# Bias row sums: scaling on the scalar engine, summing by accumulating DMAs, one addition on the vector engine

## The chip, the cores and the metric

The kernel runs on one core of a Trainium2 chip. The metric is the device time of one execution in microseconds (us), the median over several runs. A profile of one further execution gives the start and duration of every instruction on the tensor engine (PE for its matmuls, PEld for its weight loads), the vector engine (DVE), the scalar engine (ACT), GpSimd (POOL) and the sync engine (SP, which here only issues DMAs), and of the DMA queues.

## What is computed

Two layers are applied to 4096 tokens of width 1024. In each, a first linear map (`cond`) feeds a second one (`ffn`) with low-rank experts, and the result is added to the input:

```python
x = x + _L0_ffn_ref(_L0_cond_ref(x, ...), ...)      # layer 0: weight rounded to a codebook, then W_base, b_base, experts
x = x + _L1_ffn_ref(_L1_cond_ref(x, ...), ...)      # layer 1: weight, bias, adapter per sequence, then base_W, experts

# inside _L0_ffn_ref
base = xf @ W_base.T + b_base
# inside _L1_cond_ref
base = jnp.einsum('bsi,oi->bso', x, weight) + bias
# inside _L1_ffn_ref
base = jnp.einsum('bsd,od->bso', x, base_W)
logits = jnp.einsum('bsd,ed->bse', x, router_W)
```

All linear maps between the two layers' non-linear parts are folded into products of weight matrices first, and the tokens are sent through the folded matrices. Folding also needs the two biases pushed through the matrices behind them: with M the 1024 x 1160 matrix `m1t` (base_W, the experts' A and the router of layer 1) and E the 1024 x 1288 matrix of the first folding stage, the kernel needs the row vector

`bias_sum = sum over r of bias1[r] * M[r, :] + sum over r of bias0[r] * E[r, :]`

with M's columns put at their places among E's. These are the "bias row sums".

## The kernel before, in words

Every float32 matrix product is done as three products of a high and a low part (`split_product`, L555 to L559); ACT makes a high part (`hi_of`), DVE the low part (`lo_of`). The order of the work on each engine is written out by hand, and semaphores tie the engines together. The stages, by the time at which they stand in the trace:

- 0 to 162 us: the product E, and beside it the rounding of layer 0's weight. E is stored chunk by chunk (128 rows) to `e_scratch` in device memory.
- 162 to 221 us, the C stage: for j = 0 to 7 and two halves h of 512 columns, a 1024-long product of a block of `wall` with `weff` (`c_product`) goes to one of 8 PSUM banks; ACT copies it out as `c0_hi` (the tile `c_hi` in the trace), DVE as `c0_lo` (`c_lo`). Blocks 13 to 16 of `wall` (needed by j = 4 to 7) are split by ACT and DVE behind j = 0, 1, 4 and 5 (`W_AFTER`, `w_split`: `w_hi`, `w_lo`).
- 221 to 239 us, the H stage: eight groups of matmuls, i = 0 to 7 (L725). Into groups 4 to 7 are put 22 small matmuls (eleven pairs) with a column of ones (`bias_sum`, L708) that sum `bacc` over its 128 partitions. Group 4 therefore waits for `bacc` to be finished, and it waits for `h_sum`, the first of DVE's additions `h_add` (L1672), as group i waits for the addition of group i - 4 for its PSUM bank.
- 239 to some 355 us, the G stage: further products of the folded matrices; the first reads `en_hi` and `en_lo`, made from `en_raw`, which SP loads from `e_scratch` when the bias sums are finished, since `en_raw` lies over the buffer `ea`.
- The rest: the tokens, in 16 tiles of 256.

The bias sums are made during the C stage. For each of 8 chunks k of 128 rows, POOL loads 128 rows of M into the one buffer `ma` and 128 rows of E into the one buffer `ea`. DVE multiplies each row with its bias (one number per partition) and adds it to `bacc`, [128 x 1288]: two instructions for `ma` (L1651 with 1024 columns, L1652 with 136), one for `ea` (L1656). POOL loads the next chunk when DVE has read the last one. On DVE the chunks stand behind j = 2 (one), 3 (two), 4 (one), 5 (two) and 6 (two). Behind them come the two `c_lo` of j = 7, then `b0t_lo` (the low part of another weight), then the `h_add`s.

Of the kernel before, what the change touches and what calls it, by code (L numbers as in the profile page):

```python
# [65 lines left out]
def build(nc, xq, wall, m1t, aallt, x0t, b0t, lb1, lorabt, loraa, wq, cbook, ids, packed, out,  # L66
          e_dram, p1_dram, b_dram, t_dram, p0_dram):
    with ExitStack() as ctx:
# [5 lines left out]
        def at(name, shape, dt, offset):  # L74
            return nc.alloc_sbuf_tensor_at(name, shape, dt, offset=offset)
# [53 lines left out]
        ea = at("ea", [P, NE], F32, r4 + 33280)  # L129
        ma = at("ma", [P, NM1], F32, r4 + 46880)  # L130
# [141 lines left out]
        ld_ma, ld_ea, ma_ok, mb_ok = sem("ld_ma"), sem("ld_ea"), sem("ma_ok"), sem("mb_ok")  # L272
# [13 lines left out]
        zero_ok, ids_ok = sem("zero_ok"), sem("ids_ok")  # L286
# [18 lines left out]
        fin_ok, fin_mm = sem("fin_ok"), sem("fin_mm")  # L305
# [23 lines left out]
        def _(sp):  # L329
# [55 lines left out]
            sp.wait_ge(mb_ok, KC)  # L385
# [105 lines left out]
        def _(pool):  # L491
# [12 lines left out]
            pool.dma_start(ma[:], m1t[0:P, :]).then_inc(ld_ma, 16)  # L504
# [4 lines left out]
            pool.dma_start(ea[:], e_dram[0:P, :]).then_inc(ld_ea, 16)  # L509
# [43 lines left out]
        def _(pe):  # L553
# [536 lines left out]
        def _(act):  # L1090
# [348 lines left out]
        def _(v):  # L1439
# [197 lines left out]
            nc.vector.memset(bacc[:], 0.0).then_inc(zero_ok, 1)  # L1637
# [6 lines left out]
            def bias(k):  # L1644
                v.wait_ge(ld_ma, 16 * k + 16)
                if k:
                    v.wait_ge(mb_ok, k)
                else:
                    v.wait_ge(zero_ok, 2)
                b = b1c[:, k:k + 1]  # L1650
# [3 lines left out]
                v.wait_ge(ld_ea, 16 * k + 16)  # L1654
                v.wait_ge(ma_ok, k + 1)
# [546 lines left out]
```

## Time and profile before

| | |
|---|---|
| median of 3 runs | 899.62 us (899.13 to 900.24) |
| the profiled execution, its own time | 899.72 us |
| its span from first to last instruction | 898.0 us |
| PE busy | 891.7 us (99%) |
| DVE busy | 673.5 us (75%) |
| ACT busy | 327.5 us (36%) |
| POOL busy | 149.1 us (17%) |
| TensorE clock granted | the highest digit in all 40 slices |

"Busy" is the share of the span in which an engine has an instruction under way. PE is busy nearly throughout, so an instruction on another engine matters where PE comes to wait for it. 1.7 us of the profiled execution lie outside its span.

### The profile page before, as it was taken

Reading aid. Unit: us, or ns where it says so; the run is one execution under the profiler, and the core shown is the slowest. Engines: PE = TensorE matmul, PEld = TensorE weight load, DVE = VectorE, ACT = ScalarE, POOL = GpSimd, SP = SyncE. Lnnn points to the kernel's source line nnn. Section 1 sums busy time; section 2 is a strip of 40 time slices with the busy share of each in tenths; the row PEclk is TensorE's granted clock in tenths of the full one; section 3 lists DMA queues with packets and bytes.
Section 4 is the critical chain, followed back from the end, with each engine's and each line's share of the span. In section 5 each row is a group of like instructions: output and inputs, shape, how many; then the busy total and the mean of one; then the engine's idle time right before and its main releaser. Section 6 shows DMA issues by size and latency. Waiting matters only on the chain.

```text
span 898.0 us, 13642 instructions
## 1 busy us (share of the span) xinstructions
PE 891.7 (99%) x4641; PEld 780.5 (87%) x4641; DVE 673.5 (75%) x1473; ACT 327.5 (36%) x546; POOL 149.1 (17%) x298
## 2 busy tenths in 40 slices
PE   8999999999999999999999999999999999999998
PEld 8999998888998888888888888888888888888887
DVE  7899899675687868888676776776776776767764
ACT  6578778411334424232322222222222222222220
POOL 0100010011002001414212312212302302302300
PEclk9999999999999999999999999999999999999999
DMA  9523330666412042575787887887887887886875
GB/s 361 194 89 109 121 127 24 215 228 201 143 51 93 2 141 83 190 278 186 233 288 244 300 298 245 293 299 247 295 284 260 299 293 246 302 292 242 304 271 207
DMA packets 61123, 192.52 MB, mean 214 GB/s; under 512 B 7777, under 2 KB 10874, under 8 KB 59134
## 3 DMA queue, kind: packets, MB, share of 16 engines
q1 hardware_dynamic: 50332, 160.04, 50.3%
q0 software_dynamic: 10432, 31.35, 11.6%
q8 instruction: 37, 0.61, 0.3%
q10 hardware_dynamic: 290, 0.26, 0.1%
q14 instruction: 32, 0.26, 0.1%
HBM read 159.39 MB, written 32.76 MB: 214 GB/s over the span
## 4 chain that ended last, share of the span: by engine, by line
PE 85%; DVE 6%; DMA 5%; ACT 2%; issue 1%; SPq 0%; DVEq 0%; ACTq 0%
PE bank L924 30%; PE bank L557 11%; PE bank L558 11%; PE bank L559 11%; PE bank L906 6%; PE bank L892 4%; DMA ea<-e_scratch 3%; PE bank L901 2%; PE bank L1017 2%; DVE bacc L1656 1%; DMA w_raw<-wall 1%; DVE rbuf L1611 1%; PE bank L725 1%; DMA m_raw<-m1t 1%; PE bank L835 1%
## 5 line engine op out<-in xcount | busy, mean ns | idle before, releaser
L924 PE MATMUL bank<-g_hi,xs 128*128 128x512 f32 x448 | 152.6, 398 | 0.0
L528 POOL DMA_DIRECT2D p1sel<-p_scratch x128 | 65.3, 510 | 340.2 <-issue 340.0
L924 PE MATMUL bank<-t_hi,xs 128*128 128x512 f32 x328 | 108.7, 392 | 0.0
L924 PEld LDWEIGHTS bank<-g_hi,xs 128*128 128x128 f32 x448 | 83.2, 188 | 15.6
L924 PE MATMUL bank<-g_lo,xs 128*128 128x512 f32 x224 | 88.3, 394 | 0.0
L1450 DVE TENSOR_TENSOR xs<-x_raw,xs 128x1024 fp32r<-128x1024 f32 x60 | 73.3, 1244 | 12.2 <-ACT xs L1093 11.9
L557 PE MATMUL bank<-gx,xs 128*128 128x304 f32 x256 | 78.5, 307 | 0.0
L559 PE MATMUL bank<-gx,xs 128*128 128x304 f32 x256 | 77.4, 302 | 0.0
L1093 ACT ACTIVATE xs<-x_raw 128x1024 fp32r<-128x1024 f32 x60 | 61.7, 1053 | 42.5 <-PE bank L924 41.8
L558 PE MATMUL bank<-gx,xs 128*128 128x304 f32 x256 | 77.2, 301 | 0.0
L924 PEld LDWEIGHTS bank<-t_hi,xs 128*128 128x128 f32 x328 | 61.6, 188 | 14.2 <-DMA t_lo<-t_scratch 0.5
L924 PE MATMUL bank<-t_lo,xs 128*128 128x512 f32 x164 | 64.0, 390 | 0.0
L1611 DVE SCALAR_TENSOR_TENSOR rbuf<-qbuf,thr,rbuf 128x1024 f32<-128x1024 f32 x48 | 59.5, 1281 | 5.0 <-ACT rbuf L1144 4.4
L557 PE MATMUL bank<-m_hi,w_hi 128*128 128x388 f32 (+1 forms) x184 | 63.0, 343 | 0.0
L558 PE MATMUL bank<-m_lo,w_hi 128*128 128x388 f32 (+1 forms) x184 | 62.3, 338 | 0.0
L559 PE MATMUL bank<-m_hi,w_lo 128*128 128x388 f32 (+1 forms) x184 | 62.2, 338 | 0.0
L539 POOL COPY bls<-bl 128x16 f32 x64 | 31.7, 495 | 179.4 <-issue 106.6
L1144 ACT ACTIVATE rbuf<-rbuf,step 128x1024 f32<-128x1024 f32 x48 | 53.8, 1148 | 10.3 <-DVE rbuf L1606 6.8
L557 PE MATMUL bank<-weff_hi,w_hi 128*128 128x512 f32 x128 | 50.3, 393 | 0.0
L559 PE MATMUL bank<-weff_hi,w_lo 128*128 128x512 f32 x128 | 49.9, 390 | 0.0
L558 PE MATMUL bank<-weff_lo,w_hi 128*128 128x512 f32 x128 | 49.8, 389 | 0.0
L924 PEld LDWEIGHTS bank<-g_lo,xs 128*128 128x128 f32 x224 | 42.2, 189 | 7.5
(404 smaller groups left out, 2101.6 us busy)
## 6 DMA issues: line engine op xcount, KB each, us to landing
t_hi<-t_scratch SPq DMA_DIRECT2D x82, 512.0 KB, 5.5
t_lo<-t_scratch SPq DMA_DIRECT2D x82, 512.0 KB, 6.6
x_raw<-xq SPq DMA_DIRECT2D x16, 1024.0 KB, 7.7
out<-ost SPq DMA_DIRECT2D x62, 256.0 KB, 7.7
p1sel<-p_scratch POOLq DMA_DIRECT2D x64, 192.0 KB, 5.8
w_raw<-wall SPq DMA_DIRECT2D x16, 512.0 KB, 4.5
w<-e_scratch SPq DMA_DIRECT2D x6, 1024.0 KB, 5.1
ea<-e_scratch POOLq DMA_DIRECT2D x8, 644.0 KB, 4.3
```

The source lines that it names most:

```text
L528: pool.dma_start(f(p1sel[b][STK * s:STK * s + STK, cs]), p1_dram[bass.ds(i * STK, STK), cs]).then_inc(sems[b], 16)
L539: nc.gpsimd.tensor_copy(bls[:, b, s, :], bl[:, i, :].squeeze(1))
L557: nc.tensor.matmul(out_ap, lhs_hi, rhs_hi, start=first, stop=False, skip_group_check=True)
L558: nc.tensor.matmul(out_ap, lhs_hi, rhs_lo, start=False, stop=False, skip_group_check=True)
L559: return nc.tensor.matmul(out_ap, lhs_lo, rhs_hi, start=False, stop=last, skip_group_check=True)
L892: mm = nc.tensor.matmul(bk[j][:], l[tau][:, c, b * P:b * P + P], m[:, c, hs], start=c + k == 0, stop=c + k == KC + 1, skip_group_check=True)
L906: mm = nc.tensor.matmul(dst, l, m, start=first and k == 0, stop=k == 2, skip_group_check=True)
L924: mm = nc.tensor.matmul(bk[j][:], l[:, c, :], m[:, c, :], start=first and c + k == 0, stop=c + k == KH + 1, skip_group_check=True)
L1093: return nc.scalar.activation(dst, src, ACT.Identity)
L1144: nc.scalar.activation(rbuf[u][:], rbuf[u][:], ACT.Identity, bias=step[:, m:m + 1]).then_inc(a_ready[u], 1)
L1450: return nc.vector.tensor_tensor(dst, src, f(hi), ALU.subtract)
L1611: nc.vector.scalar_tensor_tensor(rbuf[u][:], qbuf[u][:], thr[:, m:m + 1], rbuf[u][:], ALU.is_gt, ALU.mult).then_inc(r_ready[u], 1)
```

## The change

The multiplications move from DVE to ACT (`bias_parts`), and the additions over the chunks to DMAs that add to what their destination holds (`accum_op=ALU.add`), issued by POOL. M's chunks are summed in a buffer of their own, `bm` [128 x 1160], and E's in `bacc`; chunk 0 is written there by ACT directly, and chunks 1 to 7 are scaled in place and then added by a DMA each. DVE adds `bm` to `bacc` at the end in two instructions (`bias_total`). `ma` and `ea` have two buffers each. A pair of loads for chunk k + 2 is issued when the accumulating pair of chunk k has landed and the loads of chunk k + 1 too. Some semaphores are used for a second purpose, with their counts shifted.

```diff
+BIAS_AFTER = {(1, 1): (0,), (4, 0): (1, 2), (5, 0): (3,), (5, 1): (4,), (6, 0): (5,), (6, 1): (6,), (7, 0): (7,)}
...
-            sp.wait_ge(mb_ok, KC)
+            sp.wait_ge(ea_sum, 16 * (KC - 1))
             sp.dma_start(en_raw[:], e_dram[:, D:NE].rearrange("(c p) n -> p c n", p=P)).then_inc(ld_en, 16)
...
+            def load_bias(k):
+                pool.wait_ge(ld_ma, 16 * k)
+                pool.wait_ge(ld_ea, 16 * k)
+                pool.dma_start(ma[k % 2][:], m1t[k * P:(k + 1) * P, :]).then_inc(ld_ma, 16)
+                pool.dma_start(ea[k % 2][:], e_dram[k * P:(k + 1) * P, :]).then_inc(ld_ea, 16)
+
+            pool.wait_ge(st_p1, 48)
+            load_bias(1)
+            pool.wait_ge(ma_ok, 1)
+            pool.wait_ge(ea_ok, 1)
+            load_bias(2)
             for k in range(1, KC):
-                pool.wait_ge(ma_ok, k)
-                pool.dma_start(ma[:], m1t[k * P:(k + 1) * P, :]).then_inc(ld_ma, 16)
-                pool.wait_ge(mb_ok, k)
-                pool.dma_start(ea[:], e_dram[k * P:(k + 1) * P, :]).then_inc(ld_ea, 16)
+                pool.wait_ge(ma_ok, k + 1)
+                pool.dma_start(bm[:], ma[k % 2][:], accum_op=ALU.add).then_inc(ma_sum, 16)
+                pool.wait_ge(ea_ok, k + 1)
+                pool.dma_start(bacc[:], ea[k % 2][:], accum_op=ALU.add).then_inc(ea_sum, 16)
+                if k + 1 < KC:
+                    pool.wait_ge(ma_sum, 16 * k)
+                    pool.wait_ge(ea_sum, 16 * k)
+                if k + 2 < KC:
+                    load_bias(k + 2)
...
                 if i == 4:
-                    pe.wait_ge(mb_ok, KC)
+                    pe.wait_ge(bsum_ok, KC // 2 + 1)
                     pe.wait_ge(c_lo, 2 * KC)
...
+            def bias_parts(k):
+                act.wait_ge(ld_ma, 16 * k + 16)
+                nc.scalar.activation(ma[k % 2][:] if k else bm[:], ma[k % 2][:], ACT.Identity,
+                                     scale=b1c[:, k:k + 1]).then_inc(ma_ok, 1)
+                act.wait_ge(ld_ea, 16 * k + 16)
+                nc.scalar.activation(ea[k % 2][:] if k else bacc[:], ea[k % 2][:], ACT.Identity,
+                                     scale=b0c[:, k:k + 1]).then_inc(ea_ok, 1)
+
             for j in range(KC):
                 for h in range(2):
                     act.wait_ge(b_mm, 2 * j + h + 1)
                     hi_of(c0_hi[:, j, halves[h]], c_bank(j, h)[:]).then_inc(c_hi, 1)
+                    for k in BIAS_AFTER.get((j, h), ()):
+                        bias_parts(k)
                 if j in W_AFTER:
                     w_split(W_AFTER[j])
             act.wait_ge(ld_b0t, 16)
-            act.wait_ge(mb_ok, KC)
+            act.wait_ge(ea_sum, 16 * (KC - 1))
             hi_of(b0t_hi[:], b0t_raw[:]).then_inc(af_hi_s, 1)
...
-            nc.vector.memset(bacc[:], 0.0).then_inc(zero_ok, 1)
...
-            def bias(k):
-                ...
-                nc.vector.scalar_tensor_tensor(bacc[:, 0:D], ma[:, 0:D], b, bacc[:, 0:D], ALU.mult, ALU.add)
-                nc.vector.scalar_tensor_tensor(bacc[:, MID0:NE], ma[:, D:NM1], b, bacc[:, MID0:NE],
-                                               ALU.mult, ALU.add).then_inc(ma_ok, 1)
-                ...
-                nc.vector.scalar_tensor_tensor(bacc[:], ea[:], b0c[:, k:k + 1], bacc[:],
-                                               ALU.mult, ALU.add).then_inc(mb_ok, 1)
-
-            done = 0
+            def bias_total():
+                v.wait_ge(ma_sum, 16 * (KC - 1))
+                v.wait_ge(ea_sum, 16 * (KC - 1))
+                nc.vector.tensor_tensor(bacc[:, 0:D], bacc[:, 0:D], bm[:, 0:D], ALU.add)
+                nc.vector.tensor_tensor(bacc[:, MID0:NE], bacc[:, MID0:NE], bm[:, D:NM1], ALU.add).then_inc(bsum_ok, 1)
+
             for j in range(KC):
                 c0_out(j)
                 if j in W_AFTER:
                     w_split(W_AFTER[j])
-                for _ in range((0, 0, 1, 2, 1, 2, 2, 0)[j]):
-                    bias(done)
-                    done += 1
+            bias_total()
```

POOL's queue of DMAs during the C stage, before, from the load of chunk 0's rows of E on (`p_scratch` is a store of another table; the last two rows come seven times):

```order
L509 DMA ea<-e_scratch 128x1288 [waits st_e,st_low,p1s_lo_s,p1s_hi_s]
L511 DMA p_scratch<-p1s_hi 128x1160
L512 DMA p_scratch<-p1s_lo 128x1160
L513 DMA p_scratch<-p1s_hi 128x1160
L516 DMA ma<-m1t 128x1160 [waits ma_ok]
L518 DMA ea<-e_scratch 128x1288 [waits mb_ok]
```

The same queue after the change, from behind those stores on (the numbers tell the two buffers apart: 107 and 105 hold even chunks, 108 and 106 odd ones):

```order
L520 DMA ma_108<-m1t 128x1160 [waits ld_ea,ld_ma,st_p1]
L521 DMA ea_106<-e_scratch 128x1288
L520 DMA ma_107<-m1t 128x1160 [waits ld_ma,ld_ea,ea_ok,ma_ok]
L521 DMA ea_105<-e_scratch 128x1288
L530 DMA bm<-ma_108 128x1160 [waits ma_ok]
L532 DMA bacc<-ea_106 128x1288 [waits ea_ok]
L520 DMA ma_108<-m1t 128x1160 [waits ld_ma,ld_ea,ea_sum,ma_sum]
L521 DMA ea_106<-e_scratch 128x1288
L530 DMA bm<-ma_107 128x1160 [waits ma_ok]
L532 DMA bacc<-ea_105 128x1288 [waits ea_ok]
```

Where a chunk had two DMAs it now has four, two loads and two accumulating ones, and each pair of loads stands behind the accumulating pair of the chunk two before it.

ACT from the split of block 15 on, before (`c_hi` is a copy out of the C stage, `w_hi` a block of `wall`):

```order
L1093 ACTIVATE w_hi_88<-w_raw_86 128x1024 [waits b_mm,ld_w1]
L1093 ACTIVATE c_hi<-bank 128x512 [waits b_mm] x2
L1093 ACTIVATE w_hi_87<-w_raw_85 128x1024 [waits b_mm,ld_w0]
L1093 ACTIVATE c_hi<-bank 128x512 [waits b_mm] x4
L1093 ACTIVATE b0t_hi<-b0t_raw 128x1024 [waits mb_ok,ld_b0t]
```

and after, from the same place to chunk 5:

```order
L1112 ACTIVATE w_hi_88<-w_raw_86 128x1024 [waits b_mm,ld_w1]
L1112 ACTIVATE c_hi<-bank 128x512 [waits b_mm]
L1205 ACTIVATE ma_108<-ma_108,pk 128x1160 [waits ld_ma]
L1208 ACTIVATE ea_106<-ea_106,pk 128x1288 [waits ld_ea]
L1112 ACTIVATE c_hi<-bank 128x512 [waits b_mm]
L1205 ACTIVATE ma_107<-ma_107,pk 128x1160 [waits ld_ma]
L1208 ACTIVATE ea_105<-ea_105,pk 128x1288 [waits ld_ea]
L1112 ACTIVATE w_hi_87<-w_raw_85 128x1024 [waits b_mm,ld_w0]
L1112 ACTIVATE c_hi<-bank 128x512 [waits b_mm]
L1205 ACTIVATE ma_108<-ma_108,pk 128x1160 [waits ld_ma]
L1208 ACTIVATE ea_106<-ea_106,pk 128x1288 [waits ld_ea]
```

The high part of block 16 (`w_hi_87`) now stands behind chunk 4's scaling.

DVE at the end of the C stage, before and then after:

```order
L1651 SCALAR_TENSOR_TENSOR bacc<-ma,pk,bacc 128x1024 [waits mb_ok,ld_ma]
L1652 SCALAR_TENSOR_TENSOR bacc<-ma,pk,bacc 128x136
L1656 SCALAR_TENSOR_TENSOR bacc<-ea,pk,bacc 128x1288 [waits ma_ok,ld_ea]
L1450 TENSOR_TENSOR c_lo<-bank,c_hi 128x512 [waits c_hi] x2
L1450 TENSOR_TENSOR b0t_lo<-b0t_raw,b0t_hi 128x1024 [waits af_hi_s]
L1672 TENSOR_TENSOR hx_all<-bank,hx_all 128x136 [waits h_cp] x4
```

```order
L1480 TENSOR_TENSOR c_lo<-bank,c_hi 128x512 [waits c_hi] x4
L1676 TENSOR_TENSOR bacc<-bacc,bm 128x1024 [waits ea_sum,ma_sum]
L1677 TENSOR_TENSOR bacc<-bacc,bm 128x136
L1480 TENSOR_TENSOR b0t_lo<-b0t_raw,b0t_hi 128x1024 [waits af_hi_s]
L1689 TENSOR_TENSOR hx_all<-bank,hx_all 128x136 [waits h_cp] x4
```

The sum's last addition now stands behind the `c_lo`s and directly ahead of `b0t_lo` and the `h_add`s, and waits for the last two accumulating DMAs.

## Rows read from the trace of the kernel before

**Rows 1.** The page: span, and the granted clock by slice.
```profile
span 898.0 us, 13642 instructions
...
PEclk9999999999999999999999999999999999999999
```
**Rows 2.** Waits of PE in the whole span: us in total, times, longest us.
```profile
PE bank L599 <- DVE warm L1486: 1.5, 1, 1.5
PE bank L615 <- ACT m_hi L1093: 0.8, 1, 0.8
PE bank L725 <- DVE hx_all L1672: 0.5, 1, 0.5
```
**Rows 3.** Timeline of PE, H stage: start us, us, line, form [idle before <-releaser].
```profile
229.01 0.37 PE L725 MATMUL bank<-x_hl,weff_hi 128*128 128x272 f32 x1 [0.49 <-DVE hx_all L1672]
```
**Rows 4.** Timeline of DVE, end of C stage.
```profile
224.68 1.56 DVE L1656 SCALAR_TENSOR_TENSOR bacc<-ea,pk,bacc 128x1288 f32<-128x1288 f32 x1 [2.30 <-DMA ea<-e_scratch]
226.16 1.28 DVE L1450 TENSOR_TENSOR c_lo<-bank,c_hi 128x512 fp32r<-128x512 f32 x2
227.43 1.23 DVE L1450 TENSOR_TENSOR b0t_lo<-b0t_raw,b0t_hi 128x1024 fp32r<-128x1024 f32 x1
228.57 0.91 DVE L1672 TENSOR_TENSOR hx_all<-bank,hx_all 128x136 f32<-128x136 f32 x4
```
**Rows 5.** Instructions on `bacc`: duration ns min/median/max, first and last start us.
```profile
L1651 DVE SCALAR_TENSOR_TENSOR bacc<-ma,pk,bacc x8: 1275/1285/1286, 178.7 to 220.8; 128x1024 f32<-128x1024 f32 x8
L1652 DVE SCALAR_TENSOR_TENSOR bacc<-ma,pk,bacc x8: 352/353/355, 179.8 to 222.0; 128x136 f32<-128x136 f32 x8
L1656 DVE SCALAR_TENSOR_TENSOR bacc<-ea,pk,bacc x8: 1558/1560/1561, 180.3 to 224.7; 128x1288 f32<-128x1288 f32 x8
```
**Rows 6.** Timeline of ACT, 160 to 221 us, some rows.
```profile
160.51 1.16 ACT L1093 ACTIVATE p1s_hi<-est 128x1160 fp32r<-128x1160 f32 x1
...
182.44 0.60 ACT L1093 ACTIVATE c_hi<-bank 128x512 fp32r<-128x512 f32 x1 [4.21 <-PE bank L559]
...
199.51 1.05 ACT L1093 ACTIVATE w_hi<-w_raw 128x1024 fp32r<-128x1024 f32 x1
...
210.02 0.60 ACT L1093 ACTIVATE c_hi<-bank 128x512 fp32r<-128x512 f32 x1 [4.97 <-PE bank L559]
215.46 0.60 ACT L1093 ACTIVATE c_hi<-bank 128x512 fp32r<-128x512 f32 x1 [4.84 <-PE bank L559]
```
**Rows 7.** DMA issues, 160 to 262 us: KB each, median us to landing.
```profile
ea<-e_scratch POOLq DMA_DIRECT2D x8, 644.0 KB, 4.3
ma<-m1t POOLq DMA_DIRECT2D x7, 580.0 KB, 4.0
...
p_scratch<-p1s_hi POOLq DMA_DIRECT2D x2, 580.0 KB, 11.3
...
en_raw<-e_scratch SPq DMA_DIRECT2D x1, 1056.0 KB, 5.2
```
**Rows 8.** Timeline of POOL: DMA issues.
```profile
165.38 0.53 POOL L513 DMA_DIRECT2D p_scratch<-p1s_hi  x1
180.68 0.55 POOL L516 DMA_DIRECT2D ma<-m1t  x1 [14.77 <-DVE bacc L1652]
```
**Rows 9.** DMA issues, 41 to 52 us: a store from on-chip memory.
```profile
e_scratch<-est POOLq DMA_DIRECT2D x1, 512.0 KB, 2.9
```
**Rows 10.** Stretches: busy time of PE, PEld, DVE, ACT, POOL, then PEclk, DMA share, GB/s.
```profile
10.00:20.00 10.00, 9.86 (x55) 9.22 (x54) 9.23 (x8) 7.68 (x8) 0.00 (x0) 1.00 1.02 413
182.00:210.00 28.00, 28.00 (x126) 23.22 (x125) 19.09 (x21) 4.89 (x7) 4.85 (x9) 1.00 0.66 203
```
**Rows 11.** DMA queue of POOL, 186.5 to 226 us: packets, MB, share of 16 engines.
```profile
q0 software_dynamic: 1739, 7.55, 60.5%
```
**Rows 12.** Timeline of DVE: an addition of two buffers in SBUF.
```profile
157.15 2.36 DVE L1625 TENSOR_TENSOR qbuf<-d_half,rbuf 128x1024 f32<-128x1024 f32 x2
```
**Rows 13.** Timeline of PE, first microseconds.
```profile
1.46 4.53 PE L599 MATMUL bank<-warm 128*128 128x388 f32 x13 [1.46 <-DVE warm L1486]
8.80 0.69 PE L615 MATMUL bank<-m_hi,w_lo 128*128 128x388 f32 x3
...
9.33 1.22 PE L604 MATMUL bank<-m_lo,w_hi 128*128 128x388 f32 x6
```

More of the change, by code:

```diff
@@ L128, in build @@
         lb_hl = at("lb_hl", [P, D], F32R, r1 + 81920)
-        ea = at("ea", [P, NE], F32, r4 + 33280)
-        ma = at("ma", [P, NM1], F32, r4 + 46880)
+        ea = [at("ea0", [P, NE], F32, r4 + 33280), at("ea1", [P, NE], F32, r1 + 78720)]
+        ma = [at("ma0", [P, NM1], F32, r4 + 46880), at("ma1", [P, NM1], F32, r1 + 83872)]
+        bm = at("bm", [P, NM1], F32, r4)
         p0_hi = at("p0_hi", [P, D], F32R, r4)
@@ L271, in build @@
         st_p1, p1s_hi_s, p1s_lo_s = sem("st_p1"), sem("p1s_hi_s"), sem("p1s_lo_s")
-        ld_ma, ld_ea, ma_ok, mb_ok = sem("ld_ma"), sem("ld_ea"), sem("ma_ok"), sem("mb_ok")
+        ld_ma, ld_ea, ma_ok, ea_ok = sem("ld_ma"), sem("ld_ea"), sem("ma_ok"), sem("ea_ok")
+        ma_sum, ea_sum = sem("ma_sum"), sem("ea_sum")
         b_mm, c_hi, c_lo = sem("b_mm"), sem("c_hi"), sem("c_lo")
@@ L285, in build @@
         cols_mm, cols_ok = sem("cols_mm"), sem("cols_ok")
-        zero_ok, ids_ok = sem("zero_ok"), sem("ids_ok")
+        zero_ok, ids_ok, bsum_ok = sem("zero_ok"), sem("ids_ok"), q_tail
         ld_x, x_hi_s, x_lo_s = sem("ld_x"), sem("x_hi_s"), sem("x_lo_s")
@@ L304, in build @@
         s_raw_s, s_hi_s, s_lo_s = sem("s_raw_s"), sem("s_hi_s"), sem("s_lo_s")
-        fin_ok, fin_mm = sem("fin_ok"), sem("fin_mm")
+        fin_ok, fin_mm = comp_ok, cols_mm
         k_raw_s, k_hi_s, k_lo_s = sem("k_raw_s"), sem("k_hi_s"), sem("k_lo_s")
@@ L503, in _ @@
                 pool.wait_ge(d_mm[u], KC // 2)
-            pool.dma_start(ma[:], m1t[0:P, :]).then_inc(ld_ma, 16)
+            pool.dma_start(ma[0][:], m1t[0:P, :]).then_inc(ld_ma, 16)
             pool.wait_ge(p1s_hi_s, 1)
@@ L508, in _ @@
             pool.wait_ge(st_low, 16)
-            pool.dma_start(ea[:], e_dram[0:P, :]).then_inc(ld_ea, 16)
+            pool.dma_start(ea[0][:], e_dram[0:P, :]).then_inc(ld_ea, 16)
             p1_rows = p1_dram.rearrange("(n j) c -> n j c", j=3)
@@ L1642, in c0_out @@
                     lo_of(c0_lo[:, j, halves[h]], c_bank(j, h)[:], c0_hi[:, j, halves[h]]).then_inc(c_lo, 1)
-            def bias(k):
[L1645 to L1650, printed above, removed]
-                nc.vector.scalar_tensor_tensor(bacc[:, 0:D], ma[:, 0:D], b, bacc[:, 0:D], ALU.mult, ALU.add)
-                nc.vector.scalar_tensor_tensor(bacc[:, MID0:NE], ma[:, D:NM1], b, bacc[:, MID0:NE],
-                                               ALU.mult, ALU.add).then_inc(ma_ok, 1)
-                v.wait_ge(ld_ea, 16 * k + 16)
-                v.wait_ge(ma_ok, k + 1)
-                nc.vector.scalar_tensor_tensor(bacc[:], ea[:], b0c[:, k:k + 1], bacc[:],
-                                               ALU.mult, ALU.add).then_inc(mb_ok, 1)
-            done = 0
+            def bias_total():
[3 more added lines that the diff above has]
+                nc.vector.tensor_tensor(bacc[:, MID0:NE], bacc[:, MID0:NE], bm[:, D:NM1], ALU.add).then_inc(bsum_ok, 1)
             for j in range(KC):
@@ L2133, in _ @@
             out_sum(NT2 - 1, 1, bk[1], u4_sum)
-            v.wait_ge(fin_ok, 3)
+            v.wait_ge(fin_ok, 2 + 3)
             for j in (2, 3):
@@ L2138, in _ @@
                 qs = slice(256 * q, 256 * q + 256)
-                v.wait_ge(fin_mm, q + 1)
+                v.wait_ge(fin_mm, 3 + q + 1)
                 last = bk[3][:, qs] if q else xb[:, 1, qs]
```

## The prediction, written before the changed kernel was run

> **What bounds the kernel now.** I read the page first: PE is busy for nearly the whole span of 898.0 us, at the highest granted clock in every slice [rows 1]. So only what makes PE wait can be won, and the view of PE's waits shows how little that is: 1.5 and 0.8 us at the start, and a single 0.5 us wait in the part that the change touches, for DVE's addition `h_add` [rows 2]. It stands at 229.01 us, ahead of group 4 of the H stage [rows 3]. The timeline of DVE tells what made that addition late: the last multiply-and-add of the bias sums runs from 224.68 us to 226.24, having waited 2.30 us for its load, then come two `c_lo`, `b0t_lo` and the first `h_add`, and PE goes on [rows 4]. From the end of `bacc` to PE's restart are 229.01 - 226.24 = 2.8 us. PE reached group 4 at 229.01 - 0.49 = 228.5.
>
> So the bias sums are already the last thing to arrive, but by only 0.49 us. If they came arbitrarily early, the kernel would gain 0.49 us, 0.05% of its time. Everything that follows asks when they would come.
>
> **What goes.** DVE loses 8 x (1.285 + 0.353 + 1.560) = 25.6 us of work [rows 5], and the clearing of `bacc`. In the C stage PE waits for nothing [rows 2], so this is worth only the 0.49 us above.
>
> **What comes on DVE.** One addition of 1024 columns, 2.36 / 2 = 1.2 us [rows 12], and one of 136 columns, at most the 0.35 us of the multiply-and-add of that width [rows 5], taken as 0.3. They take the place of the two `c_lo` (1.3 us) in the chain behind `bacc`, as those are now done before. With L the time at which the last accumulating DMA has landed, PE restarts at L + 1.5 + (2.8 - 1.3) = L + 3.0. The change then moves the end by L + 3.0 - 229.0 = L - 226.0 us, and never below -0.49. ACT's `b0t_hi` and SP's load of `en_raw` wait for the same L; `en_raw` lands 5.2 us later [rows 7], and its two parts are needed only behind PE's groups 4 to 7, which begin later as well, so it stays hidden.
>
> **What comes on ACT.** Eight pairs of scalings. 1160 columns took 1.16 us [rows 6]; 1288 columns are scaled up from it to 1.28. ACT had work for 4.89 us in 182 to 210 us [rows 10], so the 2.4 us per chunk fit. But ACT works in order: chunk 4's pair stands ahead of the high part of block 16, which ran at 199.51 us and is needed when j = 7 begins, at 210.02 [rows 6]. With 1.05 us for it and 1.2 for DVE's part, chunk 4 must be scaled by about 207.7.
>
> **What comes on the DMA queue, and the chain through it.** Here the forecast is decided. POOL's order is: loads of chunk k + 2, accumulates of chunk k + 1, wait until both accumulates have landed, loads of chunk k + 3, and so on. All four DMAs are in POOL's one queue, the accumulates behind 1.25 MB of loads that nobody needs yet. So one chunk takes, from landing to landing: 0.3 us until POOL is released, the latency of a DMA, the data of the two loads, and the data of the two accumulates.
>
> The terms: a load of 644 KB landed after 4.3 us, one of 580 KB after 4.0, `en_raw` (1056 KB, 1.08 MB) after 5.2 [rows 7], and a store from on-chip memory of 512 KB after 2.9 [rows 9]. The best sustained rate in the trace is 413 GB/s [rows 10]; POOL's queue alone moved 7.55 MB in 60.5% of 39.5 us, 316 GB/s [rows 11]. At 413 GB/s `en_raw` leaves a latency of 5.2 - 2.6 = 2.6 us, the store 2.9 - 1.3 = 1.6. I take the middle, 2.1, and 413 GB/s, since four DMAs stand back to back. A pair (0.594 + 0.659 MB) then is 3.0 us of data.
>
> What an accumulate costs no row shows. Its ends: below, as much as a load, 3.0 us a pair (nothing suggests that it could be cheaper than moving the bytes); above, three times that, 9.1 us. It reads its source and its destination and writes one of them, so for each byte that arrives it reads two where a load reads one. I take twice a load, 6.1 us a pair.
>
> The Trainium skill has a price for this, in "Collectives: The Full Stack", section "The bandwidth ceiling: the fold count and why AG ≠ RS ≠ AR": a reducing transfer ran at half the rate of a copying one, not for the addition but for the second read. By it the pair would be 6.1 us, by the bytes that land alone 3.0; no run here shows either.
>
> The sum: the stores to `p_scratch` land at 165.38 + 11.3 = 176.7 us [rows 7, 8], and only then may POOL load chunk 1, because its new buffers lie over what is stored. That pair lands by about 182.0, and the pair of chunk 2 is issued. ACT scales chunk 1 from 183.0 (behind the copy at 182.44 [rows 6]) to 185.5, its accumulates queue behind the loads of chunk 2 and land at 182.0 + 2.1 + 3.0 + 6.1 = 193.2. Five chunks with loads ahead of them (2 to 6) take 0.3 + 2.1 + 3.0 + 6.1 = 11.5 us each: 250.7. The seventh has no loads ahead: 0.3 + 2.1 + 6.1 = 8.5, so L = 259.2. Before, a chunk took some 6 us (from 180.3 to 224.7 in seven steps, 6.3 each [rows 5]). The change costs 259.2 - 226.0 = 33.2 us.
>
> ACT's late scaling of chunk 4 shows on the way: its loads are issued at about 193.2 + 11.5 + 0.3 = 205.0, land near 209.5, and block 16 is ready about 214 instead of 203. PE stands some 4 us at the start of j = 7, but that shortens the later wait by as much and adds nothing. ACT's copies and `c_lo`s behind it come late as well, all before L.
>
> **The clock.** The 13 first matmuls of 388 columns took 4.53 us, 0.35 each, which is the spacing of the 1.2 GHz level, and later ones of that width stand (9.33 - 8.80) / 3 = 0.18 apart, the 2.4 GHz level, though PEclk reads 1.00 in every slice [rows 1, 13]. Before the slow ones PE had done nothing. A wait of over 20 us ahead of group 4 should bring the lower level back: between nothing and 13 x 0.17 = 2.2 us, taken as 1.5.
>
> The Trainium skill, "TensorE: Matmul & The Clock Gate", section "What's actually happening", says that an idle array falls back to the lower level and leaves it after a few microseconds of work; the first matmuls agree. By it the cost would be within the same 2.2 us.
>
> In all 33.2 + 1.5 = 34.7 us on the profiled execution's 899.72 (0.10 above the median shown): 934.4, given as 934.
>
> **Rivals.**
> - *Accumulates cost what loads cost.* For it: the bytes that land are the same. Against it: the second read. Chunk 1 lands at 182.0 + 2.1 + 6.0 = 190.1, a period is 0.3 + 2.1 + 6.1 = 8.5, chunk 6 at 232.6, L = 232.6 + 5.4 = 238.0: 12.0 + 1.5 us more, 913.
> - *Accumulates cost three loads or more*, because adding in flight breaks up the stream or POOL needs longer to issue them. Period 14.5, chunk 1 at 196.2, chunk 6 at 268.7, L = 280.2: 54.2 + 1.5 more, 955. Nothing in the trace speaks for it, nothing excludes it.
> - *The other side: the loads ahead cost the accumulates nothing*, as if the two kinds used different paths, and an accumulating pair lands 4.3 us after its second issue, like a load of `ea`. Its place is POOL's wait for the landing. Then a period is 0.3 + 3 x 0.54 + 4.3 = 6.2 us, chunk 1 lands at 185.6 + 4.3 = 189.9, chunk 6 at 220.9, L = 226.0: no change, 899.7. At 3.9 us the gain is the full 0.49 us, 899.2, since ACT's chunk 7 is then scaled by 215.46 + 0.60 + 2.4 = 218.5 [rows 6] in time. It decides from a landing under 4.3 us. For it: DMA engines were busy for only 66% of 182 to 210 us [rows 10]. Against it: 2.5 MB in 6.2 us would be 404 GB/s of landed bytes alone, the best rate of the trace, without a second read.
>
> **How the numbers follow.** Twice a load: 0.50; as a load: 0.25; three times or more: 0.12; no cost of the loads ahead: 0.13. The forecast is 934, its own range 922 (latency 1.6, less of the second read) to 950 (the rate of [rows 11]). The range of 909 to 953 us leaves out the last rival and the most of the third. A measurement of this kernel can tell 0.2%, 1.8 us, from no change. A gain is bounded by 0.49 us and so cannot be told: faster 0.02, for what the profile hides. Within 0.2% goes the larger part of the last rival, 0.10; slower 0.88.
>
> **What would show it.** In the changed profile: PE with two waits in this stretch, a few us at the start of j = 7 and a long one ahead of group 4 of the H stage, ended by DVE's `h_add`; DVE's final addition idle before it until an accumulating DMA lands, near 259 us; landings of the accumulates some 10 us after issue, loads behind them landing in 5; chunks in steps of 11.5 us; DVE's busy time lower by about 25 us and ACT's higher by 19.5. The forecast is wrong if the steps are 6 us: then the queue did not serialise them. Steps of 8.5 would say that the second read is free, steps of 14 and more that the addition itself is slow.

## The result, and the profile after

The changed kernel took 958.09 us (median of 6 runs, 956.92 to 960.50), the kernel before 898.99 us (median of 6, 898.68 to 900.24). The ratio is 1.0658, with an interval of 1.0646 to 1.0669: 59.1 us slower, where 34.4 had been forecast. The profiled execution took 960.50 us.

First the page of the changed kernel: span, busy time by engine, granted clock by slice.

```profile
span 958.8 us, 13648 instructions
...
PE 904.9 (94%) x4641; PEld 792.5 (83%) x4641; DVE 649.0 (68%) x1450; ACT 347.5 (36%) x562; POOL 161.9 (17%) x312
...
PEclk9999999996756999999999999999999999999999
```

Where [rows 1] read 9 in every slice, four slices of 24 us now read less. The work did move as meant: DVE is busy for 24.5 us less (673.5 before), ACT for 20.0 more (327.5 before).

Second, the waits of PE in the whole span (us in total, times, longest), which answer to [rows 2]:

```profile
PE bank L744 <- DVE hx_all L1689: 32.9, 1, 32.9
PE bank L576 <- issue: 15.1, 2, 14.9
PE bank L618 <- DVE warm L1516: 1.5, 1, 1.5
```

The 0.49 us ahead of group 4 of the H stage have become 32.9 us, and a second wait of 14.9 us stands at the start of j = 7, line 576.

Third, the chain that ended last, between the stores to `p_scratch` and PE's restart (start us, us, what):

```profile
165.47 11.83 DMA p_scratch<-p1s_hi
...
178.31 9.07 DMA ea<-e_scratch
...
189.58 11.37 DMA bacc<-ea
200.99 0.54 issue
201.52 0.56 POOL ma L520
...
203.31 10.87 DMA bacc<-ea
...
214.75 0.56 POOL ma L520
...
257.02 10.98 DMA bacc<-ea
268.03 0.49 issue
268.52 0.55 POOL bm L530
269.07 7.49 DMA bacc<-ea
276.65 1.23 DVE bacc L1676
...
278.09 1.13 DVE b0t_lo L1480
...
279.57 1.56 PE bank L744 x6
```

It is one ring, passed six times: POOL issues the loads of one chunk and the accumulates of another, an accumulate into `bacc` lands some 11 us later, and only then is POOL released. Five steps from 201.52 to 268.52 us are 13.4 us each. The last accumulate lands at 276.6, and PE restarts at 279.57, 3.0 us later. Before, it restarted at 229.01 [rows 3]. So 50.6 of the 60.8 us that the span grew are there at PE's restart. The other 10.2 come behind it.

Fourth, what lies inside one step (columns as in [rows 10]):

```profile
201.50:203.00 1.50, 1.50 (x9) 1.22 (x8) 0.00 (x0) 0.00 (x0) 1.37 (x3) 1.00 0.18 25
203.00:207.00 4.00, 4.00 (x19) 3.33 (x18) 0.00 (x0) 0.84 (x1) 1.57 (x2) 1.00 0.97 289
208.00:213.00 5.00, 2.49 (x12) 1.74 (x10) 0.69 (x1) 1.85 (x2) 0.00 (x0) 1.00 1.04 210
213.00:214.20 1.20, 0.00 (x0) 0.00 (x0) 0.00 (x0) 0.00 (x0) 0.00 (x0) 0.77 0.08 13
```

The last column tells it: 1.5 us in which almost nothing moves, the loads, then a plateau of 210 GB/s while only accumulates are left, with the DMA engines fully busy (share 1.04), and 1.2 us from the last data to the landing. At 210 GB/s the 1.253 MB of the two accumulates take 6.0 us; 4.0 of the 10 us of data are left for the loads. That split is worked out and not seen directly: around 206 to 208 us the end of the loads and the start of the accumulates overlap.

Fifth, the H stage behind the restart, of the changed kernel:

```profile
279.50:298.40 18.90, 18.82 (x87) 18.69 (x88) 3.78 (x8) 2.91 (x5) 0.00 (x0) 0.50 0.28 90
300.00:302.00 2.00, 2.00 (x11) 2.00 (x11) 1.49 (x3) 0.35 (x1) 0.00 (x0) 0.50 0.93 311
304.00:306.00 2.00, 2.00 (x19) 2.00 (x18) 2.00 (x3) 0.00 (x0) 0.00 (x0) 1.00 0.00 0
```

and of the kernel before, the same 86 or 87 matmuls:

```profile
229.00:239.10 10.10, 10.09 (x86) 9.98 (x87) 3.62 (x8) 2.80 (x5) 0.00 (x0) 1.00 0.49 158
```

The seventh column is the granted clock: 0.50, the 1.2 GHz level, for the whole stage, where it was 1.00. That is 8.8 us, and as the level comes back only after 302 us, what follows the stage bears the other 1.4 of the 10.2. What brings it back are matmuls that are no wider than those of the H stage. PE's timeline, the first of the G stage and the first that is quick again:

```profile
298.29 0.52 PE L576 MATMUL bank<-en_hi,b0t_hi 128*128 128x264 f32 x1
302.35 0.32 PE L576 MATMUL bank<-en_hi,b0t_hi 128*128 128x264 f32 x1
```

Matmuls of 264 columns, one every 0.22 us, had run for 4 us when the level rose. The H stage has a pair of 272 and 136 columns every 0.44 us and matmuls of 1 column between them, and ran 18.9 us without a rise.

### The profile page after: what moved, and what is told of

Its sections match the earlier page's. It is cut to its first block, busy times and chain, and to the rows that moved or that the text cites. A ratio compares the mean times of both kernels' runs of the same rounds, so it can differ in the third digit from the quotient of the medians.

```text
span 958.8 us, 13648 instructions
## 1 busy us (share of the span) xinstructions
PE 904.9 (94%) x4641; PEld 792.5 (83%) x4641; DVE 649.0 (68%) x1450; ACT 347.5 (36%) x562; POOL 161.9 (17%) x312
## 3 DMA queue, kind: packets, MB, share of 16 engines
q0 software_dynamic: 12448, 40.12, 15.7%
## 4 chain that ended last, share of the span: by engine, by line
PE 81%; DMA 11%; DVE 4%; ACT 2%; POOL 1%; issue 1%; SPq 0%; DVEq 0%; POOLq 0%; ACTq 0%
PE bank L943 28%; PE bank L576 11%; PE bank L578 11%; PE bank L577 11%; DMA bacc<-ea 8%; PE bank L925 6%; PE bank L911 4%; PE bank L920 2%; PE bank L744 2%; PE bank L1036 2%; DMA p_scratch<-p1s_hi 1%; DVE rbuf L1641 1%; DMA ea<-e_scratch 1%; DMA m_raw<-m1t 1%; PE bank L854 1%
## 5 line engine op out<-in xcount | busy, mean ns | idle before, releaser
L558 POOL COPY bls<-bl 128x16 f32 x64 | 34.8, 543 | 188.7 <-issue 116.8
L744 PE MATMUL bank<-x_hl,weff_hi 128*128 128x272 f32 x64 | 23.3, 440 | 32.9 <-DVE hx_all L1689 32.9
L1480 DVE TENSOR_TENSOR c_lo<-bank,c_hi 128x512 fp32r<-128x512 f32 x16 | 10.6, 685 | 63.0 <-ACT c_hi L1112 63.0
```

Source lines behind the costliest of these rows:

```text
L744: mm = nc.tensor.matmul(bk[i % 4][:, 0:n], w[:, c, i * P:(i + 1) * P], x0_hl[:, c, 0:n], start=c + k == 0, stop=c + k == KC, skip_group_ch ...
L1480: return nc.vector.tensor_tensor(dst, src, f(hi), ALU.subtract)
```

## The experiments

Theories. **A (ring and clock)**: the loss is POOL's ring, 13.4 us a chunk, in which loads and accumulates share one set of DMA engines and an accumulate moves at about half the rate of a plain copy; and behind the long wait the H stage runs at the lower clock, 10 us more. **Rivals**: the accumulates are slow by latency or by POOL's issue, not by rate; the queue's order is what costs; ACT's scaling or DVE's addition is what costs; the clock is only a companion of the wait.

### e1_plain_copies: the accumulates become plain copies

```diff
-                pool.dma_start(bm[:], ma[k % 2][:], accum_op=ALU.add).then_inc(ma_sum, 16)
+                pool.dma_start(bm[:], ma[k % 2][:]).then_inc(ma_sum, 16)
...
-                pool.dma_start(bacc[:], ea[k % 2][:], accum_op=ALU.add).then_inc(ea_sum, 16)
+                pool.dma_start(bacc[:], ea[k % 2][:]).then_inc(ea_sum, 16)
```

> The changed kernel with the fourteen accumulating DMAs turned into plain copies over the same bytes (the sum over the chunks is left out). Theory 'bytes': POOL's chain sets the end, a step is 4.3 us of release, issue and latency + 3.0 us for two loads + 6.0 us for two accumulates, because the accumulates move data at half the rate (second read). Plain copies then take 3.0 us a pair: steps of 10.4 us in place of 13.4, last landing near 255 us in place of 276.6, 936 us in all. Rival 'latency': the pair is slow by POOL's longer issue and the way to landing, not by data; then the steps stay at 13.4 and the time at 958.

938.86 us (938.68 to 939.04), ratio 1.0438 (1.0408 to 1.0469). The sum over the chunks is left out here. The chain, cut to the start of the first of five steps and its end (start us, us, what):

```profile
196.44 0.54 POOL ma L520
...
198.22 8.32 DMA bacc<-ea
...
250.14 0.53 POOL bm L530
250.67 4.09 DMA bacc<-ea
254.85 1.23 DVE bacc L1676
...
257.78 1.56 PE bank L744 x6
```

Five steps from 196.44 to 250.14: 10.7 us each, 2.7 less than with accumulates. Where copies were under way the rate was 389 GB/s:

```profile
202.00:205.00 3.00, 3.00 (x15) 2.50 (x14) 0.00 (x0) 1.44 (x2) 0.00 (x0) 1.00 0.97 389
```

The difference goes with the rate of the data, not with a fixed latency: at 389 GB/s the pair is 3.2 us, at 210 it is 6.0. POOL's longer issue of an accumulate does not make it either: in the changed kernel POOL had issued all four DMAs of the step by 204.6 us, and the data flowed until 213. And even with plain copies the kernel loses 40 us: PE restarts at 257.78, 28.8 us later than before, and the span is 39.0 us longer, so the lower clock costs its 10.2 us here too. So of the 50.6 us at PE's restart 21.8 went with the accumulates, 2.6 of them because the ring started earlier in this execution (185.35 instead of 187.96 us): the accumulate's rate is the smaller part of the loss.

### e2_no_loads: only chunks 0 to 2 are loaded, their buffers are scaled and accumulated again

```diff
                     pool.wait_ge(ea_sum, 16 * k)
-                if k + 2 < KC:
-                    load_bias(k + 2)
...
-                act.wait_ge(ld_ma, 16 * k + 16)
+                if k > 2:
+                    act.wait_ge(ma_sum, 16 * (k - 2))
+                    act.wait_ge(ea_sum, 16 * (k - 2))
...
+                act.wait_ge(ld_ma, 16 * min(k, 2) + 16)
```

> The changed kernel without the loads of chunks 3 to 7; ACT scales the two buffers again instead (the data of five chunks is left out, all accumulates stay). Theory 'bytes in one queue': without loads ahead a step is what the last one was, 8.5 us; the six steps from chunk 2 to 7 end near 252 us in place of 276.6, 934 us in all. Rival 'landing alone': the accumulates' own latency sets the step and the loads ran in its shadow; then 13 us a step remain and 958 us.

935.25 us (934.87 to 935.62), ratio 1.0398 (1.0368 to 1.0428). The chain, start of the first of five steps and its end:

```profile
199.85 0.55 POOL bm L530
...
243.61 0.55 POOL bm L530
```

That is 8.75 us each. So the loads that nobody needs yet cost, with their two issues, 13.4 - 8.75 = 4.65 us of every step, though they are overlapped in the program: they and the accumulates move one after the other. With the 2.7 us of e1 that explains 7.4 of 13.4; the rest is release, latency and what the bytes of two plain copies take.

### e3_loads_on_sp: the same loads, issued by SP instead of POOL

```diff
+            for k in range(1, KC):
+                if k > 2:
+                    sp.wait_ge(ma_sum, 16 * (k - 2))
+                    sp.wait_ge(ea_sum, 16 * (k - 2))
...
+                sp.dma_start(ma[k % 2][:], m1t[k * P:(k + 1) * P, :]).then_inc(lm, 16)
+                sp.dma_start(ea[k % 2][:], e_dram[k * P:(k + 1) * P, :]).then_inc(le, 16)
```

> The changed kernel with the loads of chunks 1 to 7 issued by SP on its own queue, with the same waits. Theory 'order in the queue': accumulates then never stand behind loads, a step falls from 13.4 to 8.5 or 9 us, 935 us in all. Rival 'shared engines': both queues run on the same 16 DMA engines, 9 us of data per step remain, only 1.1 us of POOL's issues go: steps of 12 us, 950 us.

953.73 us (953.14 to 954.33), ratio 1.0604 (1.0573 to 1.0635); steps of 12.8 us. Another queue gives back 0.6 us of a step, which is no more than the two issues of 0.54 us that POOL is spared. What the two kinds of transfer share is behind the queues. The DMA engines, fully busy in the rows above, are the likely place; no run tells them from another shared part.

### e4_accumulates_first: each chunk's accumulates are issued ahead of the next loads

```diff
             for k in range(1, KC):
+                if k > 1:
+                    pool.wait_ge(ma_sum, 16 * (k - 1))
+                    pool.wait_ge(ea_sum, 16 * (k - 1))
                 pool.wait_ge(ma_ok, k + 1)
...
-                if k + 2 < KC:
-                    load_bias(k + 2)
+                if 1 < k < KC - 1:
+                    load_bias(k + 1)
```

> The changed kernel with POOL issuing the accumulates of chunk k ahead of the loads of chunk k + 1 (k from 2), each after the landing of chunk k - 1. Theory 'bytes in one queue': the accumulates land 8.5 us after the step begins, but the loads behind them are needed by the next step: issue 0.5, accumulates 6.0, loads 3.0, latency 3, scaling 2.6, so about 15 us to the next accumulates and 8.5 to their landing, two chunks in 24 us, 12 a chunk in place of 13.4: 950 us. Rival 'order does not matter': 958.

955.15 us (954.10 to 956.20), ratio 1.0620 (1.0589 to 1.0650), between the two expectations. A row of POOL's timeline, one of five alike:

```profile
237.29 0.88 POOL L533 DMA_DIRECT2D bm<-ma  x1 [10.46 <-ACT ma L1205]
```

POOL no longer waits for an accumulate but for ACT's scaling of a chunk whose loads now stand behind the accumulates. The ring keeps nearly its length, 12.8 us, with another member last. The order does not matter while every step carries both pairs.

### e5_act_scales_dve_adds: ACT scales as in the change, DVE adds each chunk, no accumulating DMA

```diff
-                pool.dma_start(bm[:], ma[k % 2][:], accum_op=ALU.add).then_inc(ma_sum, 16)
-                pool.dma_start(bacc[:], ea[k % 2][:], accum_op=ALU.add).then_inc(ea_sum, 16)
...
                 if k + 2 < KC:
+                    pool.wait_ge(ea_sum, k)
                     load_bias(k + 2)
...
-            bias_total()
+                for _ in range((0, 0, 1, 0, 2, 2, 2, 1)[j]):
+                    bias(done)
+                    done += 1
```

> ACT scales the chunks as in the changed kernel, two buffers each, but DVE adds them to bacc with tensor additions and no accumulating DMA is issued. Theory: the accumulating DMAs are the whole loss; the bias sums are then in time, PE's 0.49 us wait goes, 898.5 us, a ratio to before of 0.9995. Rival 'the scalar engine': scaling ahead of the copies and of block 16 delays PE; then over 901 us.

925.47 us (923.90 to 928.38, 6 runs), ratio 1.0287 (1.0250 to 1.0324): the expectation failed by 27 us. ACT's and DVE's timelines around 192 us, and POOL's:

```profile
191.59 1.37 ACT L1202 ACTIVATE ea<-ea,pk 128x1288 f32<-128x1288 f32 x1 [0.29 <-DMA ea<-e_scratch]
192.87 0.58 ACT L1106 ACTIVATE c_hi<-bank 128x512 fp32r<-128x512 f32 x1
```

```profile
193.48 0.69 DVE L1474 TENSOR_TENSOR c_lo<-bank,c_hi 128x512 fp32r<-128x512 f32 x1 [9.72 <-ACT c_hi L1106]
...
195.57 1.22 DVE L1676 TENSOR_TENSOR bacc<-ma,bacc 128x1024 f32<-128x1024 f32 x1
```

```profile
198.90 0.54 POOL L520 DMA_DIRECT2D ma<-m1t  x1 [11.82 <-DVE bacc L1681]
...
217.48 0.54 POOL L520 DMA_DIRECT2D ma<-m1t  x1 [11.31 <-DVE bacc L1681]
```

Chunk 1 was scaled by 186.8, but DVE added it only at 195.57: in DVE's order the addition stood behind the second `c_lo` of j = 4 (and the `w_lo` after it), which waited for `c_hi` on ACT, which in ACT's order stood behind the scaling of chunk 2. POOL waited 11.8 us for that addition before it could load chunk 3. Two in-order engines with the same work in a different order had made a ring of their own. The clock followed again: PE waited 10.4 us ahead of group 4, and the 87 matmuls of the 18.8 us behind ran at 0.50.

### e9_adds_beside_scales: as e5, each chunk's additions right behind the `c_lo` that follows its scaling

The edit, against e5:

```diff
                     lo_of(c0_lo[:, j, halves[h]], c_bank(j, h)[:], c0_hi[:, j, halves[h]]).then_inc(c_lo, 1)
+                    for k in BIAS_AFTER.get((j, h), ()):
+                        bias(k)
...
-                for _ in range((0, 0, 1, 0, 2, 2, 2, 1)[j]):
-                    bias(done)
-                    done += 1
```

> e5_act_scales_dve_adds with DVE's additions of a chunk put behind the same copy as ACT's scaling of it (before, they stood behind both copies of a block). e5 took 925 us, against the 898.5 expected. Theory 'crossed order': there DVE added chunk 1 only behind a copy that on ACT stood behind chunk 2's scaling, so that POOL reloaded chunk 1's buffer 12 us late, three times over. With the additions beside the scalings a step is a pair of loads, some 6.2 us, bacc is ready by 226 and the whole takes 899. Rival 'ACT waits for loads in line with its copies': the step stays at 8 us or more whatever DVE's order, and the whole over 905.

899.39 us (898.65 to 901.15, 10 runs), ratio 1.0003 (0.9994 to 1.0013). DVE's last addition:

```profile
224.18 1.50 DVE L1683 TENSOR_TENSOR bacc<-ea,bacc 128x1288 f32<-128x1288 f32 x1 [0.29 <-ACT ea L1202]
```

The sums are ready at 225.7, half a microsecond before [rows 4], chunks come in steps of 6 to 7 us, and PE's wait is gone. So 20 us of scaling on ACT, two buffers and the same chunks cost nothing. What costs is who adds them up.

### e6_two_buffers_only: the kernel before, with two buffers each and nothing else

```diff
-                pool.wait_ge(ma_ok, k)
-                pool.dma_start(ma[:], m1t[k * P:(k + 1) * P, :]).then_inc(ld_ma, 16)
...
+                if k > 1:
+                    pool.wait_ge(ma_ok, k - 1)
+                pool.wait_ge(ld_ma, 16 * k)
+                pool.dma_start(ma[k % 2][:], m1t[k * P:(k + 1) * P, :]).then_inc(ld_ma, 16)
```

> The kernel before with two buffers for each load and nothing else changed (DVE still multiplies and adds). Theory: DVE no longer waits for loads, bacc is ready about 4 us earlier, PE's 0.49 us wait goes: 898.5 us, a ratio of 0.9995, which may not be told from no change. Rival 'a gain behind it': earlier loads of en_raw and of the blocks behind shorten more than the one wait; under 897.5 us.

898.84 us (898.71 to 899.92, 12 runs), ratio 0.9993 (0.9975 to 1.0011). DVE's last multiply-and-add ends at 218.06 instead of 226.24:

```profile
216.50 1.56 DVE L1662 SCALAR_TENSOR_TENSOR bacc<-ea,pk,bacc 128x1288 f32<-128x1288 f32 x1 [0.47 <-DMA ea<-e_scratch]
```

The sums are 8.2 us earlier, the wait of 0.49 us is gone, and the time cannot be told from no change. That agrees with the bound of the forecast's first step, though the interval by itself would still allow a gain of 2.2 us. Next to nothing was to be won here.

### e10_wait_filled: 154 matmuls that nobody needs fill PE's wait

```diff
                 if i == 4:
+                    pe.wait_ge(c_lo, 13)
+                    for _ in range(154):
+                        nc.tensor.matmul(bk[4][:], weff_hi[:, 0, 0:P], weff_hi[:, 0, 0:512], start=True, stop=True)
```

> e7 with 154 wide matmuls in place of 136, enough for the whole wait. In the profile of e7 PE ran at the full granted clock up to a rest of 3.5 us and then at 0.50 through the H stage; one of its four executions took 945.5 us. Theory 'the rest of the wait drops the clock': with no rest left the H stage takes 10.2 us and all runs take 946 to 950 us. Rival: the clock falls at that place for another reason; 958 us and more.

947.97 us (947.96 to 948.30, 4 runs), ratio 1.0545 (1.0528 to 1.0563). The stretch of the wait, and the H stage behind it:

```profile
247.00:277.30 30.30, 30.30 (x135) 25.12 (x134) 4.53 (x9) 5.32 (x9) 4.72 (x6) 1.00 0.75 166
277.30:287.50 10.20, 10.20 (x88) 10.00 (x87) 3.39 (x7) 2.80 (x5) 0.00 (x0) 1.00 0.47 152
```

More work for PE, and the kernel is 10 us faster than the changed one; the intervals of the ratios lie far apart. In this execution the span grew by 48.3 us over before, and the H stage began 277.59 - 229.01 = 48.6 us later: behind the restart nothing is lost any more. The 10.2 us were the clock's.

### e7_matmuls_in_the_wait: the same with 136

```diff
+                    for _ in range(136):
```

> The changed kernel with 136 matmuls of 512 columns (results unused) in front of PE's wait for the bias sums, some 31 of its 33 us. Theory 'clock': the H stage took 18.9 us in place of 10.2 because PE had waited and its clock was at the lower level; with PE busy in the wait it takes 10.2, and the whole 949 us. Rival 'the wait itself': the H stage stays slow for another reason (late data of DVE or ACT), 958 us.

957.83 us (945.51 to 959.15, 4 runs), ratio 1.0586 (1.0493 to 1.0679). The filling ended too early (PE's timeline, then two stretches):

```profile
277.65 0.56 PE L747 MATMUL bank<-x_hl,weff_hi 128*128 128x272 f32 x1 [3.49 <-DVE hx_all L1692]
```

```profile
247.00:270.00 23.00, 23.00 (x103) 19.03 (x102) 1.38 (x2) 4.14 (x5) 4.72 (x6) 1.00 0.74 165
...
280.00:290.00 10.00, 10.00 (x48) 10.00 (x47) 2.94 (x4) 2.62 (x4) 0.00 (x0) 0.50 0.34 107
```

In the profiled execution a rest of 3.5 us was enough to bring back the 1.2 GHz level, and with it the clock's part of the loss. The run of 945.51 us shows a higher mean granted clock (0.993, the profiled one 0.980), the clock of e10's runs. It has no trace, so whether its rest was shorter or the level stayed in spite of it is not known.

### e8_wide_matmuls_after: 16 matmuls of 512 columns between the wait and group 4

```diff
                     pe.wait_ge(c_lo, 2 * KC)
+                    pe.wait_ge(h_sum, 1)
+                    for _ in range(16):
+                        nc.tensor.matmul(bk[4][:], weff_hi[:, 0, 0:P], weff_hi[:, 0, 0:512], start=True, stop=True)
```

> The changed kernel with 16 matmuls of 512 columns (results unused) directly behind PE's wait, ahead of group 4 of the H stage. If wide matmuls bring the clock back where the H stage's narrow ones do not, they take 16 x 0.43 = 6.9 us or less and the H stage 10.2 in place of 18.9: 956 us. If they do not, they only add their 6.9 us: 965 us.

954.15 us (953.34 to 956.06, 4 runs), ratio 1.0597 (1.0536 to 1.0659). PE's timeline, then three stretches:

```profile
276.87 6.32 PE L739 MATMUL bank<-weff_hi 128*128 128x512 f32 x16 [33.01 <-DVE hx_all L1692]
```

```profile
279.00:282.00 3.00, 3.00 (x8) 2.32 (x8) 1.76 (x2) 2.06 (x2) 0.00 (x0) 0.50 0.00 0
282.00:284.00 2.00, 2.00 (x14) 1.75 (x14) 0.67 (x1) 0.00 (x0) 0.00 (x0) 0.99 0.28 32
284.00:293.00 9.00, 9.00 (x78) 8.88 (x78) 0.90 (x3) 0.85 (x3) 0.00 (x0) 1.00 0.33 111
```

The level is back about 5 us behind the wait and the H stage takes its 10.2 us, at the price of the 6 us put in. PE is busy in the rows of the changed kernel too (18.82 of 18.90 us), with matmuls of 272, 136 and 1 columns, and there the level stayed at 0.50. So the profile's busy share does not tell whether the level will rise. Nor does the width of the single matmul: those of 264 columns behind the H stage raised it as well.

### e11_block16_first: ACT converts block 16 ahead of chunk 4's scaling

```diff
+                    if (j, h) == (5, 1):
+                        w_split(W_AFTER[5])
                     for k in BIAS_AFTER.get((j, h), ()):
                         bias_parts(k)
-                if j in W_AFTER:
+                if j in W_AFTER and j != 5:
```

> The changed kernel with ACT splitting block 16 ahead of chunk 4's scaling. PE's wait of 15 us at the start of j = 7 goes. Theory 'only the last landing counts': the wait ahead of group 4 grows by the same 15 us and the time stays at 958 (957 to 959). Rival 'the late copies cost of themselves': about 15 us less, 943.

959.64 us (958.56 to 960.72), ratio 1.0674 (1.0652 to 1.0695). PE's waits:

```profile
PE bank L744 <- DVE hx_all L1691: 48.6, 1, 48.6
PE bank L576 <- issue: 1.6, 1, 1.6
```

14.9 us of wait at j = 7 had become 1.6, the wait at group 4 grew by 15.7, and the time cannot be told from the changed kernel's. A wait ahead of a later and longer one cost nothing here: PE's arrival there does not set the end.

## Why the prediction was wrong in size

**What held.** The bound of 0.49 us on any gain (e6). The chain: POOL's ring, the last accumulate, DVE's addition, `b0t_lo`, `h_add`. PE's restart at L + 3.0, to a tenth. DVE's busy time 24.5 us lower (25 forecast), ACT's 20.0 higher (19.5). Two waits of PE in the places named, the first worth nothing (e11), though it was 14.9 us and not 4: chunk 4's loads came 10 us late by the same longer steps.

The price of an accumulate, the term with the widest bounds and the one taken by judgement, was right: 6.0 us a pair against 6.1, 210 GB/s against half of the 413 in [rows 10]. The number is confirmed, the reason given for it (a second read) is not. Two of the rivals fall with it: as a load (913), and three times (955), whose time lies near the measured one while its mechanism is not what happened. "No cost of the loads ahead" falls to e2 and e3. The Trainium skill, "Collectives: The Full Stack", section "The bandwidth ceiling: the fold count and why AG ≠ RS ≠ AR", gives a reducing transfer of a collective half the rate of a copying one. This kernel agrees, for transfers inside one core's memory (210 GB/s against the 389 of e1). Whether it is the second read or the addition no run here tells.

**What failed: the other terms of the step.** The forecast was 0.3 + 2.1 + 3.0 + 6.1 = 11.5 us; the step from 200.99 to 214.21 us was

| term | forecast | measured |
|---|---|---|
| until POOL is released | 0.3 | 0.54 |
| latency, start and end | 2.1 | 1.5 + 1.2 = 2.7 |
| data of the two loads | 3.0 | 4.0 (the rest of 10 us) |
| data of the two accumulates | 6.1 | 6.0 (1.253 MB at 210 GB/s) |
| sum | 11.5 | 13.2 (mean of five 13.4) |

The latency was taken as the middle of 1.6 and 2.6 us, and the upper end would have been right. The loads were put at the best rate in the trace, 413 GB/s, with the argument that four DMAs stand back to back; but each step begins from an empty queue. The 4 us from 203 on moved 289 GB/s, with the engines busy for 0.97 of them: 158 GB/s in the first half microsecond, never above 359 later. How much of this is the start and how much the accumulates that begin before the loads have ended, the rows do not separate. The row of POOL's own queue, 316 GB/s [rows 11], was in view, would have given 4.0 us, and was used only for the range. (With that rate for both pairs the forecast's own sum comes to 953 us, not to the 950 that it gives as its upper end.) Five steps, 9.5 us late.

**The start.** 182.0 us was forecast for the landing of chunk 1, from the 4.3 us of a load by itself; it landed at 187.4. Its `ea` took 9.07 us from issue (4.3 in [rows 7]): the two loads went out together and `b0t_raw`'s 512 KB, issued by SP at 178.44, went with them; 0.6 us of the delay had come before, with the landing of the stores (177.30 instead of 176.7). Part of it belongs to this execution: in e1, e2, e4, e7, e8, e10 and e11, where POOL starts the same way and SP issued `b0t_raw` at 176.8 to 177.5 us, POOL went on at 185.1 to 186.0 us instead of 187.96. No run tests `b0t_raw`'s share by itself. 5.4 us, and the first step, longer by 2.3 for the reasons above. Together L = 259.2 + 5.4 + 2.3 + 9.5 = 276.4, measured 276.6.

**The clock.** The forecast took [rows 13] as the price of a cold start: 13 matmuls at 0.35 instead of 0.18 us, at most 2.2 us, after which the level returns. It cost 10.2 us (e10), because all 87 matmuls of the H stage, and those behind it up to 302 us, ran at the lower level. The first 13 matmuls had 388 columns and stood close together; the H stage's did not bring the level back. e8 shows the difference with the wait left as it was. The Trainium skill, "TensorE: Matmul & The Clock Gate", section "What's actually happening", has the fall after idleness, which e7 confirms, and has the level rise again once the array works. The matmuls of 264 columns and those of e8 agree with that second part; the 18.9 us in which the profile has PE busy at 0.50 do not, and the measurement decides.

The ledger: 34.7 us forecast, 17.4 for L and 8.7 for the clock make 60.8, the growth of the span. Some nine of these 26 us were within sight as the upper ends of two terms (2.6 us of latency, and 4.0 us for the loads by [rows 11], over six turns); but these were taken at their middle and at their best, and errors of one sign add up over the turns of the ring. Another eight or so are the late start and the rest of the steps, and the last nine came from a mechanism that was named and sized from matmuls of another shape.

**Still open.** Why the H stage's matmuls do not raise the level. Their largest width is not it, as 264 columns were enough behind them; the narrow ones among them (136 and 1 columns), gaps that the weight loads leave, or another property are left. Whether much shorter waits can cost a stage in the same way: two of the 40 executions of the kernel before that were run beside the experiments took 908.2 and 908.7 us at a mean granted clock of 0.991, the others 0.998 to 1.000, and no trace of the two was kept. Whether the half rate is the second read or the addition. And none of the eleven variants beats the kernel before: the best two, e6 and e9, cannot be told from it.

## What to carry to other kernels

A pair of accumulating DMAs (1.25 MB) saves DVE additions of 3.0 us (1.22, 0.29 and 1.50 us in e5) and takes 6.0 us of all DMA engines, plus the latency at the start and end of the ring that it closes. By these numbers it is a saving only where the engines are idle and nobody waits for the landing. When a ring is to be forecast, its length is the sum of every member on the way, each taken from a row in the same situation (an empty queue, a pair issued together), and an error of 1.9 us is multiplied by the number of turns. And a new wait of TensorE is charged twice: once for itself, and once for what stands behind it until the level is back (here 8.8 us for the H stage, nearly its own 10.1 us once more, and 1.4 us for what follows it). How soon the level returns has to be read from rows of the same matmuls.

## What the runs showed of the hardware

- An accumulating DMA from on-chip to on-chip memory moved 210 GB/s with the DMA engines fully busy, plain copies 389 (e1). POOL needs longer to issue it, 0.93 and 1.28 us against 0.54 for a plain copy (e1).
- Loads on another queue hardly help: 12.8 us a step against 13.4 (e3).
- A rest of TensorE of 3.5 us brought back the 1.2 GHz level in the profiled execution of e7; 16 matmuls of 512 columns raised it again within about 5 us (e8), 87 of 272, 136 and 1 columns did not in 18.9 us, and those of 264 columns behind them did in 4 us. Putting useless wide matmuls into the wait gained 10 us (e10).
- Multiplying by a scale per partition took ACT 1.26 us for 1160 columns and 1.37 for 1288, where a conversion of 1160 columns took 1.16 [rows 6].
